# Graph network kernel: the scaling of x goes to GpSimd, and VectorE makes part of the first-value operands

## The reference

```python
deg_out = jnp.clip(jax.ops.segment_sum(ones_e, src, num_segments=N), 1.0)
norm_src = jax.lax.rsqrt(deg_out)[:, None]
h = X * norm_src
agg = jax.ops.segment_sum(h[src], dst, num_segments=N)
```

## Time and profile before

| | us |
|---|---|
| median of 3 runs | 3874.34 |
| lowest, highest | 3874.33, 3883.9 |
| the profiled execution | 3883.49 |
| its span | 3881.8 |

### The profile page before, as it was taken

One profiled execution on the slowest core, in us unless ns is written; L12 is line 12 of the kernel. 1 busy time (PEld: TensorE's weight loads), 2 busy tenths in 40 slices (PEclk: granted clock), 3 DMA queues, 4 the chain that ended last, 5 costly groups with the idle time before them and its releaser, 6 DMA issues. The chain is left out here.

```text
span 3881.8 us, 90523 instructions
## 1 busy us (share of the span) xinstructions
PE 3040.9 (78%) x22958; PEld 2646.1 (68%) x22958; DVE 3053.6 (79%) x9551; ACT 2635.1 (68%) x5985; POOL 1740.6 (45%) x1684
## 2 busy tenths in 40 slices
PE   4966536666699787776899998988867999986665
PEld 3743325565555566665799998777767999986555
DVE  9999746566699899995567777999955677779998
ACT  3789718788544577774567775666644677759999
POOL 0000167777000244445777751444457777502332
PEclk9999968678899899998999999999989999988999
DMA  0047513445588799995456765888853566647886
GB/s 19 2 141 226 170 47 88 104 124 132 154 288 282 245 346 334 333 333 202 123 165 204 216 212 170 289 278 278 279 182 115 171 199 217 211 165 236 266 267 207
DMA packets 460974, 777.90 MB, mean 200 GB/s; under 512 B 113720, under 2 KB 115896, under 8 KB 460680
## 3 DMA queue, kind: packets, MB, share of 16 engines
q1 hardware_dynamic: 379912, 594.12, 46.8%
q0 software_dynamic: 37632, 77.15, 7.9%
q10 hardware_dynamic: 43136, 102.98, 7.7%
HBM read 438.91 MB, written 334.88 MB: 199 GB/s over the span
## 5 line engine op out<-in xcount | busy, mean ns | idle before, releaser
L861 DVE SCALAR_TENSOR_TENSOR edges_acc<-edges_acc,keep,edges_ps_a 128x128 f32 (+1 forms) x2352 | 819.5, 348 | 344.4 <-issue 142.1
L829 POOL DMA_INDIRECT ring<-table_p,esrc x784 | 787.5, 1004 | 269.5 <-issue 206.7
L949 PE MATMUL edges_ps_m<-ring,ident 128*128 x3136 | 622.8, 281 | 111.3 <-issue 40.6
L1262 ACT ACTIVATE nodes_z<-nodes_y,nodes_shift,nodes_rstd 128x128 f32<-128x128 f32 x1176 | 486.9, 492 | 268.2 <-DVE nodes_shift L1393 267.3
L950 PE MATMUL edges_ps_m<-edges_q_ring,edges_turned 128*128 x3136 | 618.7, 280 | 0.0
L1221 POOL TENSOR_TENSOR nodes_extra<-ub,deg 128x512 f32<-128x512 f32 x196 | 203.7, 1039 | 869.8 <-DVE nodes_b_out L1417 446.7
L949 PEld LDWEIGHTS edges_ps_m<-ring,ident 128*128 128x128 f32 x3136 | 486.7, 196 | 120.4 <-issue 84.9
L917 ACT ACTIVATE edges_msg<-edges_ps_m 128x512 f32<-128x512 f32 x392 | 234.0, 597 | 406.8 <-PE edges_ps_m L950 406.8
L950 PEld LDWEIGHTS edges_ps_m<-edges_q_ring,edges_turned 128*128 128x128 f32 x3136 | 488.2, 196 | 0.0
L971 PE MATMUL edges_ps_a<-ring,edges_onehot 128*128 x1568 | 301.2, 355 | 189.0 <-DVE edges_acc L861 116.0
L846 DVE TENSOR_TENSOR edges_onehot<-iota,drel 128x512 f32<-128x512 f16 x392 | 270.8, 692 | 207.6 <-PE edges_ps_a L959 207.3
(11 more groups left out here) (291 smaller groups left out, 6414.3 us busy)
## 6 DMA issues: line engine op xcount, KB each, us to landing
table_q<-nodes_q_out ACTq DMA_DIRECT2D x196, 256.0 KB, 3.6
table_p<-nodes_p_out SPq DMA_DIRECT2D x196, 256.0 KB
table_b<-nodes_b_out SPq DMA_DIRECT2D x196, 256.0 KB, 2.9
edges_q_ring<-table_q SPq DMA_DIRECT2D x196, 256.0 KB
edges_d_ring<-table_d ACTq DMA_DIRECT2D x98, 512.0 KB
table_t<-edges_acc SPq DMA_DIRECT2D x196, 256.0 KB
nodes_in_a<-table_t SPq DMA_DIRECT2D x196, 256.0 KB
nodes_in_c<-table_b SPq DMA_DIRECT2D x196, 256.0 KB, 3.4
```

The costliest lines, as they stand in the source:

```text
L829: nc.gpsimd.indirect_dma_start(out=ring[:, e % RE * W:e % RE * W + P], out_offset=None, in_=table[:, :], in_offset=bass.IndirectOffsetOnAx ...
L861: nc.vector.scalar_tensor_tensor(out=to, in0=to, scalar=m.keep[:, s:s + 1], in1=ps_a[:, i % AR, where(j):where(j) + F], op0=ALU.mult, op1= ...
L949: nc.tensor.matmul(to, m.ident[:], rows[j], start=True, stop=False)
L1262: nc.scalar.activation(dst[:, b, j * D:(j + 1) * D], src[:, b, j * D:(j + 1) * D], ACT.Identity, scale=rstd[:, b % 2, j, :], bias=shift[:, ...
```

## The change

GpSimd executes the 98 scales, in order, after its memset; they leave VectorE's order. Of the eight `val1` operands of a group the first VU = 3 are made by VectorE directly from the iota, with a comparison and a multiplication in one tensor_scalar, between L438 and L445 and behind the wait for TensorE; ScalarE makes the other five and all eight `val2`. Buffers, semaphores and DMAs stay as they were.

```diff
-    R = 4
+    R, VU = 4, 3
@@ VectorE
-                def scale(c):
-                    dve.wait_ge(s_x[c % R], 16 * (c // R + 1))
-                    if c >= R:
-                        dve.wait_ge(s_out[c % R], 16 * (c // R))
...
                     nc.vector.tensor_tensor(hot_p[:, g % 2, :, :], ...
-                    scale(2 * g)
                     if g >= 2:
                         dve.wait_ge(s_put, g - 1)
+                    for u in range(VU):
+                        t = g * SG + u
+                        nc.vector.tensor_scalar(val1[:, g % 2, u, :], m.iota[:, 0:P], m.pos_low[:, t:t + 1], m.v1[:, t:t + 1], ALU.is_equal, ALU.mult)
                     for u in range(SG):
                         t = g * SG + u
                         last = nc.vector.tensor_scalar(hot_q[:, g % 2, u, :], m.iota[:], m.pos_high[:, t:t + 1], None, ALU.is_equal)
                     last.then_inc(s_hot_q, 1)
-                    scale(2 * g + 1)
@@ GpSimd
+                def scale(c):
+                    pool.wait_ge(s_x[c % R], 16 * (c // R + 1))
+                    if c >= R:
+                        pool.wait_ge(s_out[c % R], 16 * (c // R))
+                    k = parts(c)
+                    rows = lambda t: t[0:k, c % R, :].rearrange("p (j d) -> p j d", j=J)
+                    nc.gpsimd.tensor_tensor(rows(h), rows(xin), m.norm[0:k, 0, c * J:(c + 1) * J].unsqueeze(2).to_broadcast([k, J, D]),
+                                            ALU.mult).then_inc(s_h, 1)
+
                 nc.gpsimd.memset(m.ring[:].rearrange("p (r w) -> p r w", w=W)[:, :, D:W], 1.0)
+                for c in range(NC):
+                    scale(c)
@@ ScalarE
-                        nc.scalar.activation(val1[:, g % 2, u, :], hot_p[:, g % 2, u, :], ACT.Copy, scale=m.v1[:, t:t + 1])
+                        if u >= VU:
+                            nc.scalar.activation(val1[:, g % 2, u, :], hot_p[:, g % 2, u, :], ACT.Copy, scale=m.v1[:, t:t + 1])
```

## The result

The changed kernel takes 3907.1 us (median of 4 runs, 3902.2 to 3907.7) against 3874.3, ratio 1.0076 with a 95% interval of 1.0058 to 1.0093: slower, by 33 us. Forecast were 3927 us and a range of 3882 to 3962. The profiled executions have spans of 3905.8 and 3881.8 us.

A forecast was written before the change was run, and what follows sets the result against it. ScalarE was taken as the placing stage's bound. VectorE 169.5, holds by GpSimd's scales 101.9, later groups 9.9 and start 3.9 give 285.2 us in place of 232.2, +53.0: 3927 us, range 3882 to 3962.

The forecast's parts named there:

- the two parts: Placing stage: first 172 us with GpSimd's scales, 20 groups at 8.6 us; then 29 groups at ScalarE's 3.80 us.
- second rival: Placing stage: the hold is real but partial, 0.4 to 0.6 us a scale, 3865 to 3884 us; chance 0.07.
- (a): ScalarE in the placing stage: 16 copies become 13 per group, 3.80 us against 4.68.
- (b): VectorE per group: loses two scales, 1.20 us, gains three operands at 0.16 us each; 3.46 us if left alone.
- (c): Placing stage: VectorE stands still during each of GpSimd's 98 scales, 1.04 us each, 101.9 us in all.
- (d): GpSimd's scales come at the DMA engines' pace, 1.75 us a chunk, and are done after 172 us.
- the term for the later groups: 29 groups after GpSimd's scales go at ScalarE's 3.80 us, not VectorE's 3.46: 9.9 us.
- (e): SP's store-then-load order and two issues per chunk stay; the last store lands long before the last group.
- (f): TensorE's 16 matmuls take 2.9 us a group, at most 5.8 at the lower clock; put at 0, at most a few us.
- first rival: One-input VectorE instructions run beside GpSimd in the placing stage: 190 us, -42 us, 3832 us; chance 0.13.
- the third: VectorE's queue keeps GpSimd out, which gets in once per group: +78 us, 3952 us; chance 0.08.

The follow-up runs named there:

- the scales alone: Against the kernel before, only the scales move to GpSimd and ScalarE makes all sixteen operands: stage +34.3 us, 3912.3 us, ratio 1.0078.
- the doubled scales: The changed kernel with each scale made twice by GpSimd, once into an unread buffer: stage +107.5 us, 3985.8 us, ratio 1.0270 to the kernel before.
- pacing: GpSimd's scales wait for hot_p and hot_q, two per group; with all operands on ScalarE: stage -1.3 and -0.9 us, ratios 0.9957 and 0.9969.
- the best arrangement of the stage that was being tuned: The kernel before with one of eight first-value operands moved from ScalarE to VectorE, scales staying on VectorE: stage -12.0 us, 3867.4 us, ratio 0.9978.
- the paced kernel with three operands: The changed kernel with GpSimd's scales waiting for hot_p and hot_q, two per group: stage +21.3 us, 3883.6 us, ratio 1.0016 to the kernel before.
- paced kernels: Kernels with GpSimd's scales waiting for hot_p and hot_q; three, one or no operands on VectorE: ratios 1.0016, 0.9970, and 0.9957 and 0.9969.

## Why the prediction was right

Direction, mechanism and the two parts were as forecast, and the time lies within the range. The size was too large: by 20 us in the time, by 24 in the stage (+53 said, +29.0 measured). That it lies within the range is in part luck. For this mechanism the prediction gave +37 to +86 us, 3911 to 3960, and 3907 lies just below; it is the part of the second rival that the range of 3882 to 3962 took in which covers it. (The upper end had counted dearer operands in all 49 groups, though the later ones go at ScalarE's pace; it was about 6 us too high.)

- (a) ScalarE at 13 copies: 3.80 us said, 3.79 measured in the second part. 27 groups fell into it, 29 were said.
- (b) The new operands: 0.16 us said, 0.223 measured. The fixed part of a tensor_scalar was taken from float32 rows with one operand; the float16 instruction with two per-partition operands is 309 ns long, not 246. Which of the two differences does it was not tried. VectorE alone 3.65 us, not 3.46: 49 x 0.19 = 9 us more than the term.
- (c) **The price of a hold is the term that was mis-sized**: 1.04 us said. By 386.04 us VectorE had done 21 groups, 21 x 3.65 = 76.7 us of 153.0; the other 76.3 belong to 97 scales, 0.79 us each. The kernel with the scales alone gives (152.0 - 25 x 2.98)/98 = 0.79, the doubled scales 0.80. I had 0.88 as the lower end, from L1393. Single scales show what goes below it. At 312.47, where the scale came first, the next instruction starts 1.98 us after hot_p in place of 1.13, a loss of 0.85. At 305.86, where VectorE came first and the scale waited, the three operands behind it take 1.40 us in place of 0.67, a loss of 0.73; that part of the scale's own fixed time had then passed is my reading and not shown. 98 x 0.25 = 25 us less than the term of 101.9. (The upper end of 1.27 came from L1224, which I called an instruction with two dense inputs; by the code its second input is a row of 128 repeated four times. The scale behaves as L1221, with a median of 1045 ns.)
- (d) GpSimd's pace: 1.75 us a chunk said, (387.38 - 236.35)/97 = 1.56 measured, at 339 GB/s and a share of 0.98 from 240 to 380 us; the convolution stage's 284 GB/s was not the most that they move. It changes only how early the first part ends, and with (b) the term for the later groups shrinks from 9.9 to 27 x 0.14 = 3.8 us.
- (e), (f) SP's order and TensorE cost nothing. The clock fell, 0.67 to 0.91 in the first part, with TensorE idle behind VectorE, and was 1.00 from 400 us on.

Sum with the measured terms: 49 x 3.65 = 178.9, 98 x 0.79 = 77.4, 3.8, and 3.9 for the start, 264.0; the stage's compute part was 494.3 - 233.0 = 261.3 us. The error of (c), 25 us too much, was offset in part by (b), 9 too little. A scale had to cost less than 0.50 us for the change to pay; with the operands' measured price the point is (228.3 - 178.9 - 3.8)/98 = 0.47 us, and 0.79 is well over both.

The first rival (one-input instructions run beside GpSimd) is what the hot_q rows refute, 587 ns on the mean; its -42 us is what the kernel without scaling showed (-43.4). The second, a price near 0.5, is what pacing gives where VectorE waits anyway. Of the third, GpSimd kept out, nothing was seen: it got in at 1.56 us a chunk.

## What to carry to other kernels

Work that goes from VectorE to GpSimd is not off VectorE when both work on SBUF: here 0.68 us of VectorE's own instruction (0.60 in its row) became 0.79 us of standing still, and it came below 0.60 (0.49) only where VectorE was waiting anyway. Before such a move, look in any stage where both are busy for a short VectorE instruction with a long duration, and see what GpSimd did at that time. The same rows show what is already lost: a wait that lets a 0.16 us instruction go first gave 94 us in two stages, against 12 us for the best arrangement of the stage that was being tuned.

## What the runs showed that was not expected

- GpSimd's tensor_scalar of 128x128 float32 with a per-partition operand takes 599 ns at the least and 679 in the median, over half of the 1039 ns of a tensor_tensor with four times the elements; in a row without VectorE they are 0.58 us apart.
- The exclusion falls unevenly: hot_p, 1.13 us apart and with two inputs, has a median of 1215 ns in the changed kernel too, with a maximum of 2055; hot_q and the new operands carry nearly all of it. In the paced kernel with three operands hot_q was not held at all (at most 326 ns) and the new operands, which come next when a paced scale begins, had a median of 1025 ns.
- A stage with the same code took 452 to 454 us in the four profiles of paced kernels and 465 to 470 in the nine others, with the change six stages before it. The shorter time goes with shorter holds of L1393; why is unexplained. Totals of this kernel within 0.4% should be read with the spans cut by stage.
